# The products with the values of an attention kernel: three pieces in three slots, and the copy, the turn and the pair's steps one slot later

## What is computed

```
xn   = layernorm(x)
k, q, v = split(xn @ W_kqv + b_kqv)
attn = softmax(q k^T / 4 + slope_h * (j - i), causal)
att  = (attn @ v) @ W_proj + b_proj
probs = softmax(xn @ Wg); each expert takes its 512 likeliest tokens,
        each token ends with one expert
ffn  = weight * (gelu(xn @ W1[e]) @ W2[e])
out  = x + att + ffn
```

## Time and profile before

| | before |
|---|---|
| median of 3 runs | 621.96 us (614.86 to 622.96) |
| profiled execution | 613.86 us, span 612.1 us |
| PE busy | 506.6 us, 83% of the span |
| DVE busy | 405.0 us, 66% |
| ACT busy | 354.5 us, 58% |
| the 32 groups of the loop | 335.7 us, 7.79 to 13.95 us each |
| ACT idle before line 832 (the copy) | 20.5 us in 21 places |

### The profile page before, as it was taken

How to read it: one execution, slowest core, us unless ns; L and a number is a source line. 1 busy time by engine, 2 the same in 40 slices (tenths; PEclk the granted TensorE clock), 3 DMA queues, 4 the chain that set the end, 5 groups by cost and what they waited for, 6 DMA issues and landing times.

```text
span 612.1 us, 13202 instructions
## 1 busy us (share of the span) xinstructions
PE 506.6 (83%) x4807; PEld 290.9 (48%) x4807; DVE 405.0 (66%) x829; ACT 354.5 (58%) x672; POOL 311.2 (51%) x524
## 2 busy tenths in 40 slices
PE   1989996587979899898889797897898888787994
PEld 1455653233434344444334343443346767675883
DVE  5987659998897887987798976550022454444444
ACT  4455653166777776777667755666563544444443
POOL 4877534134435363544443655553621756555675
PEclk9999997559799979889899989799799988989899
DMA  8999888232324432513424325336635444444320
GB/s 262 275 237 284 295 273 274 76 112 63 106 79 123 145 96 86 176 54 118 112 87 133 109 88 198 132 129 224 211 100 122 111 101 106 106 93 100 94 71 35
DMA packets 94903, 85.59 MB, mean 140 GB/s; under 512 B 36883, under 2 KB 84883, under 8 KB 94831
## 3 DMA queue, kind: packets, MB, share of 16 engines
q1 hardware_dynamic: 82088, 59.64, 33.1%
q0 software_dynamic: 7360, 18.80, 10.3%
q10 hardware_dynamic: 5392, 6.31, 3.3%
HBM read 42.26 MB, written 37.95 MB: 131 GB/s over the span
## 4 chain that ended last, share of the span: by engine, by line
PE 50%; DVE 24%; ACT 10%; issue 7%; another core or an unknown queue 4%; POOL 3%; DMA 1%; ACTq 0%; DVEq 0%; POOLq 0%
DVE mx L989 9%; PE ps L1373 9%; PE ps L1248 7%; PE ps L1353 7%; PE ps L1535 5%; PE ps L1403 5%; ACT pr_all L857 4%; PE ps L1525 4%; PE ps L1285 3%; PE ps L1526 3%; DVE mx L984 3%; PE ps L1383 2%; PE ps L1279 2%; PE ps L1348 2%
## 5 line engine op out<-in xcount | busy, mean ns | idle before, releaser
L857 ACT ACTIVATE pr_all<-ps 128x512 f32<-128x512 f32 x320 | 179.2, 598 | 85.4 <-PE ps L1353 76.9
L989 DVE TENSOR_REDUCE mx<-ps 128x2 f32<-128x768 f32 (+1 forms) x192 | 156.7, 862 | 17.3 <-PE ps L1285 12.0
L1353 PE MATMUL ps<-qs,ks 64*128 64x384 f16 (+3 forms) x512 | 114.6, 327 | 18.2 <-ACT pr_all L857 17.6
L1373 PE MATMUL ps<-pr_all,vt 128*17 128x512 f32 (+3 forms) x1024 | 89.9, 470 | 1.6 <-ACT pr_all L857 1.3
L703 POOL TENSOR_SCALAR_AFFINE_SELECT pr_all<-pr_all 128x256 f32<-128x256 f32 (+1 forms) x168 | 70.0, 451 | 31.4 <-ACT pr_all L857 31.2
L1285 PE MATMUL ps<-ks,qs 64*128 64x128 f16 (+3 forms) x512 | 81.8, 338 | 0.0
L1535 PE MATMUL ps<-vt,pr_all 128*128 x312 | 62.9, 289 | 20.0 <-DVE pr_all L1211 16.8
L1279 PE MATMUL ps<-step,pick 64*128 64x128 bf16 (+1 forms) x640 | 59.5, 225 | 20.0 <-DVE mx L989 14.8
L1206 DVE TENSOR_TENSOR pr_all<-ps,pr_all 128x512 f32<-128x512 f32 x39 | 26.9, 691 | 67.2 <-ACT pr_all L881 35.8
L1353 PEld LDWEIGHTS ps<-qs,ks 64*128 64x128 f16 x512 | 38.0, 99 | 60.8 <-ACT pr_all L857 44.0
L1525 PE MATMUL ps<-pr_all,xnp 128*128 128x256 f16 x312 | 60.9, 288 | 4.9 <-DVE pr_all L1206 2.7
(11 more groups left out here) (195 smaller groups left out, 896.8 us busy)
## 6 DMA issues: line engine op xcount, KB each, us to landing
qs<-q_parts SPq DMA_DIRECT2D x64, 100.0 KB
ks<-k_parts SPq DMA_DIRECT2D x64, 96.0 KB
sorted_rows<-ecmp POOLq DMA_DIRECT2D x10, 516.0 KB, 6.3
k_parts<-pr_all SPq DMA_DIRECT2D x16, 256.0 KB, 2.9
q_parts<-pr_all SPq DMA_DIRECT2D x16, 256.0 KB, 2.5
w_h<-in_L_ffn_W_dram SPq DMA_DIRECT2D x16, 256.0 KB
w_l<-in_L_ffn_W_dram SPq DMA_DIRECT2D x16, 256.0 KB
expert_parts<-w_low SPq DMA_DIRECT2D x32, 128.0 KB
```

Source lines behind the costliest of these rows:

```text
L857: act.activation(dst, src, ACT.Exp, scale=SCORE).then_inc(exp_made, 1)
L989: last = dve.tensor_reduce(mx[:, n1 % 2, :, 2 * g + c, t], ps[:, 2 * (u % 2):2 * (u % 2) + 2, c0:c0 + w], AX, ALU.max)
L1353: last = pe.matmul(dst[:, c0:c0 + w], ks[rows, p, 2 * g + i, t * P:(t + 1) * P], qs[rows, p, 2 * g + i, t * P:S], start=not masked, stop=T ...
L1373: last = pe.matmul(bank[6][32 * h:32 * h + VW, t * P:S], vt[:, n, t, g * HG + h, :], pr_all[:, HG * (g % 2) + h, W_AT[t]:W_AT[t] + S - t * ...
```

## The change

The products with the values of a group are made in three pieces instead of two: block 0, block 1, and blocks 2 and 3, in three slots that follow each other. Before, they were block 0 in one slot and blocks 1 to 3 two slots later.

For all groups y up to 26 the slots are:

| y | before: pieces, copy, turn and scale, pair, pair's copy | now |
|---|---|---|
| odd | 5 and 7; 7; 10; 13; 13 | 5, 6 and 7; 8; 11; 14; 14 |
| even | 6 and 8; 8; 11; none | 7, 8 and 9; 10; 12; none |

For the groups 27 to 30 only block 1 moves, one slot earlier; their last piece, copy, turn and pair stay. The last group is not in the table and does not change.

```diff
@@ values_at
-        first, second, copy, turn, pair, pack = {
-            GROUPS - 5: (5, 7, 7, 12, 15, 14),
-            GROUPS - 4: (4, 6, 6, 11, 0, 0),
-            GROUPS - 3: (4, 6, 6, 11, 14, 12),
-            GROUPS - 2: (3, 5, 5, 9, 0, 0)}.get(y, (5, 7, 7, 10, 13, 13) if y % 2 else (6, 8, 8, 11, 0, 0))
-        pieces[own_ + first], pieces[own_ + second] = (y, (0,)), (y, (1, 2, 3))
+        first, copy, turn, pair, pack = {
+            GROUPS - 5: (5, 7, 12, 15, 14),
+            GROUPS - 4: (4, 6, 11, 0, 0),
+            GROUPS - 3: (4, 6, 11, 14, 12),
+            GROUPS - 2: (3, 5, 9, 0, 0)}.get(y, (5, 8, 11, 14, 14) if y % 2 else (7, 10, 12, 0, 0))
+        for k, blocks in enumerate(((0,), (1,), (2, 3))):
+            pieces[own_ + first + k] = (y, blocks)
```

## The result

The changed kernel takes 625.20 us (median of 20 runs, 619.08 to 628.31); 20 runs of the kernel before beside it gave 616.96 us (605.29 to 624.23). The medians are 8.2 us apart, 1.3%. The ratio on record is 1.0229, with an interval of 1.0186 to 1.0272: slower, where 0.8% faster was forecast, though whether by more than 2% is not settled. (That ratio counts only runs within 1.5% of the fastest of the same kernel, which here are 6 of the 20 of the kernel before and all 20 of the changed one, so it is larger than the quotient of the medians.) The profiled execution took 626.14 us.

What follows compares the result with a forecast made beforehand. VectorE or TensorE, by group, was taken to bound the loop, ScalarE never. Terms -1.4 + 1.4 - 0.6 - 4.5 = -5.1 us, put on the median of 621.96, gave 617 us, 0.8% faster; range 609 to 627.

Steps and rivals of the forecast that it cites:

- term 6: One more piece in 31 groups: price 0, at most 0.2 us each, 6 us.
- Term 2: Block 1 into slot 6 or 8: next unit 0.2 us later, which VectorE has in hand; 0.
- Term 1: Odd copy from slot 7 to 8: most of TensorE's 1.57 us stall goes, VectorE covers it; direct gain 0.
- Term 3: Even y, last piece behind the unit of slot 9: VectorE gets 0.2 us ahead; 1.4 us gained.
- Term 4: Later turn, scale, pair: even turn without wait, odd pair 0.8 us late, mostly hidden; 1.4 us lost, at most 5.6.
- the rival of the late pair: Slot 14 of odd y: TensorE waits for the scale behind `row_max`; 630 us, 625 at half; chance 0.15.
- Term 5: Even y's block 0 a slot later, `y_made` in slot 9: ScalarE's wait for it costs nothing.
- Term 7: Last groups, copies of y = 29 and 30: last piece half as long, 0.6 us gained.
- Term 8: Clock falls in the loop: two of three, 2.27 us each, go with the stall; 4.5 us gained, 0 to 6.8.
- the rival of the bound work: In the loop, one engine is at 93% or more; idle only moves, the clock falls elsewhere; 621 us, chance 0.30.
- The reading that TensorE is not the bound: Groups g = 2 and 3: weight loads busy only 46% in g = 3, so chains of waits bind those 14 groups.
- the rival of the chains: 14 TensorE-bound groups give half their idle time, 4.5 us more: 612 us, 609 with all falls gone; chance 0.10.

Runs made afterwards that it cites:

- e8: The change with two pieces instead of three, blocks 0 and 1, then 2 and 3, all steps late; 564.63 us, ratio 0.9979 to the kernel before.
- e15: The kernel before with only the odd groups' copy moved, from slot 7 to slot 8; 562.42 us, ratio 0.9933.
- e11: The kernel before, two pieces, with only the even groups' steps late as in the change; 565.85 us, ratio 0.9995.
- e3: The change with turn, scaling, pair and pair's copy of odd groups back in their old slots; 572.48 us, ratio 1.0123 to the kernel before.
- e12: The kernel before, two pieces, with only the odd groups' steps late as in the change; 562.22 us, ratio 0.9910.
- e5: The change run again unaltered, beside the experiments; 574.47 us, ratio 1.0154 to the kernel before.
- e4: The kernel before run again unaltered, for a second profile; 565.83 us, ratio 0.9985.
- e1: The kernel before with three pieces in three slots, up to y = 26 all other steps in their old slots; 568.28 us, ratio 1.0045.
- e2: The kernel before, still two pieces, with all other steps late as in the change, last groups unchanged; 563.82 us, ratio 0.9969.
- e6: The change with late steps for odd groups only, three pieces everywhere; 569.83 us, ratio 1.0074 to the kernel before.

## Why the prediction was wrong, point by point

**The step that failed is term 6**, the price of one more piece: 0, with 0.2 us in each of 31 groups as its upper end. It was read from TensorE's waits for issue, which show only what stands idle, not work that becomes longer. It measured 0.38 us of busy TensorE in every group of g = 2 looked at, and 1.1 to 2.1 us in batch 6. By group at full clock, e8 against the change: 8.90 to 9.20 in G = 8, 9.79 to 10.18 in G = 10, 10.06 to 10.49 in G = 11. Over all 8 batches, falls of the clock included, the 9.1 us by which the loops differ are 2.1 in g = 0, 3.9 in g = 1, 1.0 in g = 2 and 2.1 in g = 3; single batches scatter from -0.6 to +2.3 us. Term 2 had the same error: it split 1.49 us by columns into 0.75 and 0.75, and measured 0.84 and 0.85.

What the third run pays for is shown in size and place, not in its cause. The Trainium skill ("TensorE: Matmul & The Clock Gate", the part on packing small matmuls) says that a weight load overlaps matmuls in flight only if it goes to other rows of the array. By that rule products over 128 rows between scores over 64 rows pay at each border. The trace agrees in that each border costs; no run here varied the rows alone.

**Term 1** was right in mechanism: the copy waits for nothing and the stalls of 1.57 us before the scores of slot 10 are gone. That VectorE covers the gain held in the batches with the search, though G = 8 alone seems to say otherwise. Groups 8 and 9 of e15:

```profile
205.41:214.33 8.92, 7.59 (x87) 3.64 (x87) 8.60 (x22) 7.03 (x15) 3.48 (x9) 1.00 0.57 170
214.33:224.06 9.73, 7.98 (x99) 3.39 (x97) 9.44 (x27) 7.44 (x16) 6.44 (x13) 1.00 0.29 93
```

G = 8 is 0.91 us shorter than before, but VectorE's work moved on past its end: together the two take 18.65 us, and undisturbed before 9.83 + 8.98 = 18.81 (G = 5 stands for G = 9, which had a fall). The gain is real where there is no search: in G = 24, at full clock, the kernel before takes 9.40 us with VectorE busy 7.08, and e15 takes 8.53. The term looked at group 8 alone.

**Term 3** failed. VectorE's wait of 1.69 us became 1.04, but 0.36 and 0.38 us follow it in group 8 (the rows above), 1.78 in all. e11 shows the half alone: 0.9995, and 0.4 us lost in G = 10.

**Term 4.** The pair is late by 0.66 us, near the 0.8 expected, and the rival of the late pair had that right. But it decides nothing: e3 takes the wait away and keeps the time, e12 has it (from 163 to 372 us its weight loads wait 7.7 us in 8 places, its matmuls 5.3 in 4) and is faster than both kernels. That rival's sign came true for another reason. The turn of an even y was priced "no wait": its weight loads wait up to 0.4 us for the copy in 10 places there (3.8 us in all), and its matmuls not at all in that stretch; once behind it, at y = 26, they wait 3.4 us (424.81, and 0.9 us in e5). For odd y the later turn even gains: it comes behind the unit instead of ahead of it, and g = 3 goes from 10.89 to 10.06 us (e12), while e15, with the old turn, keeps 10.88.

**Term 5** held: no such wait is among the large ones. **Term 7**: the copies at the end wait for nothing now, but G = 30 went from 7.79 to 8.17 us and G = 31 from 9.78 to 9.95. In the experiments they are 6.27 and 9.96 us in the kernels with two runs (6.28 in e11) and 6.80 or 6.81 and 10.09 in those whose last groups have three: the third run again.

**Term 8** failed. In the first comparison, 8 stretches of lowered clock lie behind 140 us in the loop before and 8 after (47.8 and 37.5 us); the term counted three of the eight, and none of the 18 us at the lower level with which the loop begins. In the second it is 6 and 6 (34.1 and 27.3 us, e4 and e5). Two of the first comparison's, as windows of the changed kernel:

```profile
177.00:183.80 6.80, 6.30 (x37) 2.23 (x36) 6.26 (x19) 4.45 (x8) 1.60 (x4) 0.50 0.03 10
258.90:265.70 6.80, 6.66 (x43) 2.43 (x36) 6.51 (x18) 4.49 (x8) 3.40 (x7) 0.50 0.12 38
```

The one at 215.68 went; that of 177.0 is new, and costs some 2.7 us (G = 5 takes 13.01 us, the undisturbed G = 9 of the same kernel 10.35). The stall of 1.57 us in group 4 is gone; the longest wait of TensorE in the 12 us ahead is now one of 1.10 us for VectorE, at 176.23. The falls moved and did not go, as the rival of the bound work said. The Trainium skill ("TensorE: Matmul & The Clock Gate", "HAM oscillation — how this bites in real kernels") ties such falls to gaps in TensorE's work; here the stalls of 1.57 us were taken away and the number stayed, so the rule gave no forecast. The clock can also hide a price: in the loops of the kernel before (e4) and of e1,

```profile
122.27:444.33 322.06, 282.03 (x2961) 133.31 (x2961) 241.82 (x500) 227.36 (x422) 157.98 (x288) 0.93 0.41 126
```

```profile
122.33:444.40 322.07, 283.92 (x2961) 129.44 (x2961) 242.78 (x500) 229.36 (x422) 158.16 (x288) 0.95 0.41 126
```

the times are equal, but e1 has 17.1 us of lowered clock behind 140 us and e4 34.1. At full clock a batch of e1 takes 39.86 us (9.35 + 9.02 + 10.48 + 11.01) and one of e4 39.07 (9.83 + 8.98 + 9.37 + 10.89). By my estimate 0.8 x 7 = 5.6 us of structure, and 17 us less at a price of 2.27 for 6.83, 5.7, cancel. So the loop of e1 looked harmless by luck of the clock. The same count for the change gives 40.20 us a batch (9.20 + 10.33 + 10.18 + 10.49, e5), 1.1 x 7 = 7.9 us, less 6.8 us of lowered clock at that price, 2.3: 5.6, and the loop measured +5.5.

**The reading that TensorE is not the bound**, from its weight loads (46%), did not hold where I had doubted it: 0.38 us of added work made G = 10 longer by 0.39 (e8 to the change), with weight loads busy 4.57 of 10.18 us. The Trainium skill ("Perfetto Trace Analysis", "Identifying the Most-Contended Engine") warns of matmul busy time; in these groups, and in batch 6 (busy 1.68 us longer, 1.69 us longer in all), it was the better guide.

**The sum.** Forecast -5.1 us. In the second comparison (e4 and e5) the loop went by +5.5 us: with e2 as the middle, the late steps gave -3.7 (322.1 to 318.4; 6.8 us less of lowered clock are 2.3 of it by the estimate above) and the third run +9.2 (318.4 to 327.6, with 27.3 us of lowered clock in both). The forecast had -5.1 for the former with the clock, and 0 for the latter. The 625.2 us of the result lie inside the range of 609 to 627 by luck: the range was laid from 621.96 us, the median of three runs of the kernel before, and that of 20 is 616.96, 5.0 us lower. The sign was wrong, and all three signs of being wrong that the prediction named came true: G = 7 and 10 moved by 0.40 and 0.81 us, TensorE waited for the scaling, and the stretches of lowered clock were as many as before. (In the rival of the chains, 612 less the third fall is 610 and not 609; nothing hangs on it.)

**What stays open.** Why a run of products costs what it does at its borders. What makes the clock fall at one order of instructions and not at another, which decides how e1, e6 and e15 come out. Why the medians of the first comparison are 8.2 us apart when its two profiled loops differ by 3.8, and what made the expert part 33 us and the loop 13 us longer there with the code unchanged. Whether e12 or e15 is the better.

## What to carry to other kernels

Splitting a run of matmuls among matmuls of another shape is not free on a TensorE that is full: read its price by comparing the same work in a stretch without waits, as merged and as cut, not from the waits for issue. A step that waits is best moved alone and by one slot: here the copy alone gave 0.7% (with less lowered clock, which may be most of it), the odd steps 0.9%, and the piece that was moved with them cost more than either. A group that becomes shorter may have handed its work to the next one, so add up neighbours before calling it a gain. Before believing an equal time, or a gain, compare stretches at the same granted clock.

## What the hardware showed that I had not expected

- The time of the same products depends on how they are cut into runs: 128 x (384, 256, 128) in one run 1.49 us, in two 0.84 + 0.84; all four blocks as 1.05 + 1.49, 1.70 + 0.84, or 1.05 + 0.84 + 0.84.
- For the same order of instructions, batches 1 to 4 repeat within 0.1 us from the first comparison to the second, falls of the clock included; the falls move by whole groups when the order changes by a slot.
- Unaltered, the part behind the loop took 154.6 us in the first comparison and 121.8 in the second, and batch 6 of the loop 47.3 and 39.3.
